# State-space stage: the last doubling of the power tables shared between GpSimd and VectorE, kernel weights written by ScalarE

## The reference, cut to what matters

```
def s4d(x, log_dt, A_re, A_im, C_re, C_im, D_skip):
    Bb, L, D = x.shape
    dt = jnp.exp(log_dt)
    A = A_re + 1j * A_im
    C = C_re + 1j * C_im
    dtA = dt[:, None] * A
    dC = C * (jnp.exp(dtA) - 1.0) / A
    powers = jnp.exp(dtA[:, :, None] * jnp.arange(L))
    K = 2.0 * jnp.einsum('dn,dnl->dl', dC, powers).real
    ...
    y = jnp.fft.irfft(xf * Kf.T[None], n=n, axis=1)[:, :L]
    return y + x * D_skip
```

## Time and profile before

| | us |
|---|---|
| median of 3 runs (3921.81 to 3928.78) | 3927.72 |
| span of the profiled execution | 3923.9 |
| busy in the span: PE, DVE, ACT, POOL | 3188.6, 2978.2, 2267.9, 1587.3 |
| instructions in the span | 54505 |

### The profile page before, as it was taken

The page is one execution under the profiler, slowest core; times in us unless marked ns, Lnnn a source line. Parts: engine busy times, 40 slices in busy tenths (PEclk is TensorE's granted clock), DMA queues, the critical chain, the costliest instruction groups (busy, mean ns, idle before and its releaser), DMA issues. The chain is left out here.

```text
span 3923.9 us, 54505 instructions
## 1 busy us (share of the span) xinstructions
PE 3188.6 (81%) x17202; PEld 2121.8 (54%) x17202; DVE 2978.2 (76%) x7467; ACT 2267.9 (58%) x2921; POOL 1587.3 (40%) x1268
## 2 busy tenths in 40 slices
PE   7638768777887587877987787689999999958999
PEld 3314334444443344445865555477777777746776
DVE  7799999999999999986679998434444334469888
ACT  4579678888987788882133333133323232347876
POOL 0025556555555466555500000113332323217775
PEclk9868878888888788878999999899999999989999
DMA  8710000000000000002223333643444442330212
GB/s 318 260 42 10 10 8 10 10 12 10 10 10 10 8 10 10 12 5 90 93 54 90 83 93 83 188 129 124 129 131 129 129 129 89 113 119 15 62 54 69
DMA packets 262025, 290.53 MB, mean 74 GB/s; under 512 B 53264, under 2 KB 175782, under 8 KB 260588
## 3 DMA queue, kind: packets, MB, share of 16 engines
q1 hardware_dynamic: 243964, 259.49, 21.9%
q10 hardware_dynamic: 14736, 12.89, 1.0%
q0 software_dynamic: 3040, 14.94, 1.0%
HBM read 218.82 MB, written 68.45 MB: 73 GB/s over the span
## 5 line engine op out<-in xcount | busy, mean ns | idle before, releaser
L1119 PE MATMUL up<-ctx,attnT 128*128 128x384 f32 (+1 forms) x1664 | 717.2, 587 | 45.5 <-ACT attnT L989 45.5
L1089 PE MATMUL score<-KT,q 64*128 64x512 f32 (+1 forms) x1792 | 380.2, 518 | 336.9 <-ACT S L949 246.2
L850 DVE MAX8 both_wide<-S 128x8 f32<-128x146 f32 (+1 forms) x2816 | 601.2, 295 | 44.0 <-ACT S L949 24.7
L809 POOL TENSOR_TENSOR S<-S 128x512 f32<-128x512 f32 (+1 forms) x224 | 424.6, 1928 | 355.1 <-DVE S L855 355.1
L1119 PEld LDWEIGHTS up<-ctx,attnT 128*128 128x128 f32 (+1 forms) x1664 | 366.1, 231 | 322.0 <-issue 162.5
L855 DVE SCALAR_TENSOR_TENSOR S<-S,both_wide 128x3202 f32<-128x3202 f32 x128 | 472.8, 3757 | 14.6 <-ACT both_wide L980 14.6
L1089 PEld LDWEIGHTS score<-KT,q 64*128 64x128 f32 x1792 | 172.3, 235 | 535.1 <-ACT S L949 399.9
L949 ACT ACTIVATE S<-score 128x1024 f32<-128x1024 f32 (+1 forms) x448 | 402.7, 931 | 90.3 <-PE score L1089 90.0
L2242 DVE TENSOR_TENSOR ff_gelu<-ff_whole,ff_gelu 128x512 fp32r<-128x512 f32 x128 | 100.5, 785 | 426.6 <-ACT ff_gelu L2436 426.6
L958 ACT ACTIVATE both_wide<-S,below 128x3202 bf16<-128x3202 f32 x128 | 379.7, 2967 | 43.3 <-DVE below L890 22.5
L980 ACT ACTIVATE both_wide<-S,ebias 128x3202 f32<-128x3202 f32 x128 | 376.3, 2964 | 23.9 <-DVE S L855 13.5
(11 more groups left out here) (435 smaller groups left out, 5982.4 us busy)
## 6 DMA issues: line engine op xcount, KB each, us to landing
s_hankel<-scratch_K SPq DMA_DIRECT2D x128, 256.0 KB, 4.4
ff_w_low<-scratch_w1l SPq DMA_DIRECT2D x112, 256.0 KB, 2.6
ff_w_low<-scratch_w2l SPq DMA_DIRECT2D x112, 256.0 KB, 2.7
xt_prep<-in_x SPq DMA_DIRECT2D x8, 1024.0 KB, 8.5
scratch_xt<-xt_prep SPq DMA_DIRECT2D x8, 1024.0 KB, 8.1
both_wide<-in_ffn_w_t POOLq DMA_DIRECT2D x8, 1024.0 KB, 11.0
q<-scratch_qt SPq DMA_DIRECT2D x128, 64.0 KB, 1.9
mod_xt<-in_x_turned SPq DMA_DIRECT2D x32, 256.0 KB, 2.6
```

Of the source, the lines that this page charges most:

```text
L809: nc.gpsimd.tensor_tensor(S[:, b, 0, chunk(j)], S[:, b, 0, chunk(j)], S[:, b, 1, chunk(j)], ALU.add).then_inc(s["summed01"], 1)
L850: nc.vector.max(cand[:, h, 8 * k:8 * k + 8], S[:, b, h, k * SEG:min((k + 1) * SEG, G)])
L1089: last = nc.tensor.matmul(score[bank(p, j)][:, e, 0:w], lhsT=q[at, b, part, h // 2, :], rhs=KT[at, h // 2, chunk(j)], start=(part == 0), s ...
L1119: last = nc.tensor.matmul(up[:, 0:DV], lhsT=attnT[0:w, e, c - 4 * g, :], rhs=ctx[0:w, c, :], start=(c == 0), stop=(c == GC - 1))
```

## The change

It does four things.

1. In the last level of `table(g)`, VectorE forms only the columns 96 to 127 (from 32 to 63). GpSimd forms the columns 64 to 95 (from 0 to 31) in a new function `upper_half(g)`, in four pieces of 8 columns: two multiplications of 128 x 256, a drain, a subtraction and an addition of 128 x 128, a drain. It starts when VectorE has done the level before (`Q_low`) and ends with `Q_upper`, for which `gather(g)` on PE waits beside `Q_ready`.
2. GpSimd's order becomes: weights of part 0, `chunk_turn(0)`, `upper_half(2)`, `upper_half(3)`, then for G = 1 to 6 `upper_half(2G + 2)`, `chunk_turn(G)`, `upper_half(2G + 3)`, and `chunk_turn(7)`.
3. The kernel weights of the parts 1 to 15 are written by ScalarE, four activations after the two `Krow` copies of the part before, and ahead of its last `copy_states`.
4. The bf16 identity is made at the start of `feed_forward` and not at the start of the program (this makes room for the tile `crossed`).

```diff
+    UPPER = 8
...
+        crossed = sb("s4_crossed", [P, 2, GP, UPPER])
...
-                def kernel_weights(g):
+                def first_weights():
 
                     pool.drain()
-                    if g:
-                        pool.wait_ge(s["K_done"], g)
...
+                def upper_half(g):
+
+                    table, at, half = Q[g % RING], pairs(g), P // 2
+                    pool.wait_ge(s["Q_low"], g - 1)
+                    for first in range(0, 2 * PIECE, UPPER):
+                        source, to = table[:, :, :, first:first + UPPER], table[:, :, :, half + first:half + first + UPPER]
+                        for part, into in ((0, to), (1, crossed[:])):
+                            nc.gpsimd.tensor_tensor(into, source, W[:, LEVELS - 1, part, at].unsqueeze(1).unsqueeze(3).broadcast_to([P, 2, GP, UPPER]), ALU.mult)
+                        pool.drain()
+                        nc.gpsimd.tensor_tensor(to[:, 0], to[:, 0], crossed[:, 1], ALU.subtract)
+                        last = nc.gpsimd.tensor_tensor(to[:, 1], to[:, 1], crossed[:, 0], ALU.add)
+                        pool.drain()
+                    last.then_inc(s["Q_upper"], 1)
+
                 pool.drain()
-                kernel_weights(0)
+                first_weights()
                 chunk_turn(0)
-                for g in range(1, PARTS):
-                    kernel_weights(g)
-                    if g % 2 and g > 1:
-                        chunk_turn(g // 2)
+                upper_half(2)
+                upper_half(3)
+                for G in range(1, PARTS // 2 - 1):
+                    upper_half(2 * G + 2)
+                    chunk_turn(G)
+                    upper_half(2 * G + 3)
+                chunk_turn(PARTS // 2 - 1)
...
                         n = 1 << level
-                        for first in range(0, n, 2 * PIECE):
+                        if level == LEVELS - 1:
+                            last.then_inc(s["Q_low"], 1)
+                        for first in range(2 * PIECE if level == LEVELS - 1 else 0, n, 2 * PIECE):
...
+                def kernel_weights(g):
+
+                    for part in range(2):
+                        for e in range(2):
+                            at = slice(NS * e, NS * (e + 1))
+                            last = nc.scalar.activation(Kz[at, part, :, e:e + CHUNKS * (SIDE - 1) + 1:CHUNKS],
+                                                        root[at, part, pairs(g)].rearrange("p (r j) -> p r j", j=SIDE),
+                                                        ACT.Copy, scale=-1.0 if part else 1.0)
+                    last.then_inc(s["Kz_ready"], 1)
...
                     nc.scalar.activation(Krow[:, P - 1:P], ksp[:, 0:1], ACT.Identity, bias=skip[:, g:g + 1]).then_inc(s["K_row"], 1)
+                    if g + 1 < PARTS:
+                        kernel_weights(g + 1)
                     copy_states(g, UG - 1)
...
                     pe.wait_ge(s["Q_ready"], g + 1)
+                    if g >= 2:
+                        pe.wait_ge(s["Q_upper"], g - 1)
...
-                nc.gpsimd.tensor_copy(const["ident_bf"][:], const["ident"][:]).then_inc(ident_made, 1)
-                pool.wait_ge(ident_made, 2)
```

More of the change, by code:

```diff
@@ L1468, in s4d @@
         s = {n: sem("s4_" + n) for n in (
-            "skip_in", "row_set", "Kz_ready", "Q_ready", "turned", "QT_ready", "U_done", "UT_ready", "U_turned", "U_copied", "turn_ready",
+            "skip_in", "row_set", "Kz_ready", "Q_low", "Q_ready", "Q_upper", "turned", "QT_ready", "U_done", "UT_ready", "U_turned", "U_copied", "turn_ready",
             "K_done", "K_row", "K_stored", "h_in0", "h_in1", "h_in2", "h_in3", "h_used", "S_ready", "y_done", "yT_ready", "y_turned",
@@ L1544, in kernel_weights @@
                             last = nc.gpsimd.tensor_scalar(Kz[at, part, :, e:e + CHUNKS * (SIDE - 1) + 1:CHUNKS],
-                                                           root[at, part, pairs(g)].rearrange("p (r j) -> p r j", j=SIDE),
+                                                           root[at, part, pairs(0)].rearrange("p (r j) -> p r j", j=SIDE),
                                                            -1.0 if part else 1.0, None, ALU.mult)
@@ L1923, in feed_forward @@
         zero = sb("ff_zero", [P, DC], BF16)
+        ident_bf = sb("ff_ident_bf", [P, P], BF16)
         edge = sb("ff_edge", [1, 1])
@@ L1938, in feed_forward @@
             "out_wanted", "out_ready", "out_normed", "x_ready", "x_wanted", "x_root", "x_read", "q_ready", "q_turned", "qT_ready",
-            "xt_free", "qT_stored", "rowstep_stored", "x_stored", "x_shifted", "biased", "edges", "rowstep_ready", "rowstep_turned", "rowstep_row", "passed")}
+            "xt_free", "qT_stored", "rowstep_stored", "x_stored", "x_shifted", "ident_bf_made", "biased", "edges", "rowstep_ready", "rowstep_turned", "rowstep_row", "passed")}
         def low_loads(F):
@@ L2064, in _ @@
             def _(pool):
+                nc.gpsimd.tensor_copy(ident_bf[:], const["ident"][:]).then_inc(s["ident_bf_made"], 1)
                 nc.gpsimd.memset(edge[:], 0.0)
@@ L2529, in turn_q @@
                     n = QUAD * g + k
+                    if n == 0:
+                        pe.wait_ge(s["ident_bf_made"], 1)
                     pe.wait_ge(s["q_ready"], n + 1)
@@ L2538, in turn_q @@
                         last = nc.tensor.transpose(fl[k % 2 if g == QUADS - 1 else 1][:].bitcast(BF16)[:, c * P:(c + 1) * P], q[:, k, c * P:(c + 1) * P],
-                                                   const["ident_bf"][:])
+                                                   ident_bf[:])
                     last.then_inc(s["q_turned"], 1)
@@ L3151, in xattn_ffn @@
         const = {"ident": sb("ident", [P, P]), "ones": sb("ones", [P, 1]),
-                 "eps": sb("eps", [P, 1]),
-                 "ident_bf": sb("ident_bf", [P, P], BF16)}
+                 "eps": sb("eps", [P, 1])}
         ident_made = sem("ident_made")
```

## The result

The changed kernel takes 3961.14 us (median of 4 runs, 3957.26 to 3963.57), the kernel before 3925.35 us in the same job (4 runs): a ratio of 1.0091 with a 95% interval of 1.0077 to 1.0106, or **+35.8 us**. The prediction was 3972 us (3945 to 3992), slower with a chance of 0.86. It was right in direction, range and mechanism; the sum of +44.7 was 9 us too large. One of the 16 runs of the kernel before that stand beside the last experiments took 10168.67 us at a granted clock of 0.482, and is left out of their median.

What follows compares the result with a forecast made beforehand. DVE was taken to set the period, with 5 to 7 us a pair before PE. Growth of the tables and pairs, +45.1, less 0.3 to 0.4 at the start, gave +44.7: 3927.7 + 44.7 = 3972 us; range 3945 to 3992.

Steps and rivals of the forecast that it cites:

- T: The begin of a table's last level, where GpSimd may start; the prediction counts its steps in us from there.
- left-overs of the odd table: POOL's nine remaining instructions of an odd table slow the next table's small DVE instructions: +2.6 us.
- Taking turns: DVE and POOL alternate at SBUF reads, one for one; a piece costs DVE 1.41 us; forecast 3954 to 3985, chance 0.72.
- the +5.6 of the even table: Carry after an even table waits for turn factors behind `upper_half`: starts at T + 13.9 instead of T + 8.25.
- without a visible delay of DVE: Claim that POOL's small weights and turn factors, reading 16 to 96 elements, passed beside DVE without visibly slowing it.
- The carry waits for GpSimd: Sign in the profile: DVE gap before each even carry, ended by POOL's `s_turn`, 5 us or so each, seven of them.
- The states as the next wait: At the carry, states come 5.9 us later and DVE's and POOL's path 6.7 us later, so nearly level.
- up to 0.8 us a pair: Cost of the kernel weights on ScalarE, delaying the last `copy_states`, if the turn factors were on time.
- No delay: Rival: POOL's reads do not delay DVE, half tables run at full speed; 3920 us, not slower, chance 0.09.
- Holding for the whole instruction: Rival: the SBUF port is held for the whole instruction, pairs grow by 11.3 us; 4005 us, chance 0.06.
- Only in pauses: Rival: POOL gets in only when DVE pauses, carry at T + 15.7; 3949 us, chance 0.07.
- The best case: Most the edit could give: 4.08 us off all tables until PE is the bound; 3886 us, chance 0.05 with what lies near.

Runs made afterwards that it cites:

- the quarter: Changed kernel with turn factors ahead of the even table's share, GpSimd forming only 16 of the last 64 columns and VectorE 48; 3934.86 us, ratio 1.0020.
- the side work: Changed kernel, but VectorE forms whole tables and GpSimd runs sixteen two-input SBUF instructions a table that nobody waits for; 4010.78 us, ratio 1.0213.
- the memset run: Changed kernel with turn factors first and `upper_half` made one memset that reads nothing; 3883.15 us, ratio 0.9889.

## Why the prediction was right, and 9 us too large

The stage's own growth can be read from the starts of the tables. Within it the profiles give +36.2 us up to `gather(15)`, and the prediction's steps give +45.1. (The stage began 1.8 us earlier and what follows it took 2.8 us less, which is the size of variation between runs and part of the 0.4 us for the identity.)

| step | predicted | measured |
|---|---|---|
| DVE's half ends | T + 6.6 or 6.7 | T + 6.7 (2117.73 to 2124.40) |
| `Q_upper`, even table | T + 12.0 | T + 11.2 |
| `Q_upper`, odd table | T + 13.3 | T + 11.2 |
| T to carry, even table | 13.9, +5.6 | 13.2, +5.0 in five pairs, +4.6 in that of table 6 |
| left-overs of the odd table | +2.6 | +1.7 to +2.6, mostly +2.3 (table 6: start to T 13.26, was 10.96) |
| odd table | -1.5 | -1.3 to -2.1 (table 7: 17.75, was 19.82) |
| pair of table 6 | +6.7 | +5.2 |
| tables 2 and 3, with their left-overs | +2.2 | +1.1 |
| first pair | +4.1 | +2.5 |
| pairs 2 to 5 | +26.8 | +22.5 (5.2, 5.6, 5.7, 6.0) |
| pair 6 to T of table 15 | +8.2 | +7.1 |
| T to `gather(15)` | +3.8 | +3.1 |

- **Taking turns** held, and so did its price, 1.41 us for a piece: 1.45 measured by itself, 1.28 in the quarter. Eight instead of seven of POOL's instructions fitted into DVE's half, one sum more. That makes the rest of the share shorter, and `Q_upper` 0.8 us earlier than predicted.
- **The mis-sized term is the +5.6 of the even table.** It was 0.6 us too large, because `Q_upper` and with it the turn factors came earlier. In the pair of table 6 it was 1.0 too large: I took the carry of before at T + 8.25, which holds for five of the six even tables, but there it waited 0.51 us and began at T + 8.6. A wait that is replaced has to be taken off the price of the one that replaces it. The six even tables are 4.1 of the 9 us (29.5 instead of 33.6), and `gather(15)` is 0.7. The seven left-overs are another 2.5.
- **The rest, about 2 us, is in the odd tables and in table 4.** Up to T these tables had lasted 11.2 to 11.7 us in the kernel before, and lasted 11.0 in the changed one, but for one of 11.4. In table 7 of the kernel before, GpSimd's turn factors ran beside it, and a pair of VectorE's multiplications of 256 elements took 0.94 us there and 0.76 elsewhere. So the prediction's "without a visible delay of DVE", said of the weights and turn factors, was wrong; it bears on no term but this:

```profile
2168.61 0.94 DVE L1581 TENSOR_TENSOR s_M<-s_Q,W 128x256 f32<-128x256 f32 x2
2168.81 0.46 POOL L1557 COPY s_turn<-powers 128x96 f32<-128x96 f32 x1
```

- **The carry waits for GpSimd** was right, in place (L1639), count (seven) and releaser (`s_turn`); it was 6.5 us each, where I had written "5 us or so".
- **The states as the next wait** was right: with the turn factors first six carries wait for ACT. In the changed kernel, the last state copy ends 2.9 us ahead of the carry, so the slack was wider than the tie I described. The prediction let the gather of an odd table start at about T + 13.3, taking GpSimd's last nine instructions as slowed by VectorE; it started at T + 11.3, and the states came 2 us earlier for it. The weights' four activations (0.93 us) hid in that slack. Where the turn factors are on time they cost between 0 and 7 us in all; "up to 0.8 us a pair", 4.8 for six, is inside that.
- **DVE's multiplication** was to grow to some 1.1 us where POOL works; a round of four took 3.93 instead of 2.50 us, so about 1.0 each.
- **The rivals.** No delay (3920) is refuted by 829 ns in place of 687, and by the side work. Holding for the whole instruction (4005) would end DVE's half at T + 8.2; it ended at T + 6.7. Only in pauses (3949) would end it at T + 4.2.
- The best case, 3886, was reached at 3883 by the run whose share reads nothing.

In sum, the 35.8 us are: -42.6 that the shorter level is worth; about +15 for the turn factors behind `upper_half`; and +63 for GpSimd's reads and for its slowness together (3946.5 against 3883.2). (These add up to 35.4; the kernel before was 0.4 us apart in the two jobs.) The +63 was not split further: the same instructions both hold DVE and deliver late.

## What to carry to other kernels

Before work goes from VectorE to GpSimd, price what GpSimd's instruction takes from VectorE, not only how long GpSimd needs. Here a piece of 8 columns took 1.3 to 1.45 us from VectorE, which would have spent 1.05 on it itself, so that a share of the large columns did not pay even where nobody waited for it. What paid (-20 us) was handing over small instructions whose fixed cost is most of their time, at a place where VectorE is at small work too; the size was varied at this place, the place itself was not. And a queue has an order: what others wait for (six small copies) goes ahead of long work that is needed later; that alone was 15 us.

## What the runs showed of the hardware that I had not expected

- A GpSimd instruction with one SBUF input costs VectorE a fifth of one with two (1.2 against 5.8 us a table), although it lasts longer: 847 ns at least for `tensor_scalar` of 256 elements, 0.64 us for `tensor_tensor` alone. Whether it is the input or the kind of instruction is open.
- A GpSimd instruction that only writes costs VectorE nothing: the memset of 1024 elements lasts 0.97 us beside it, and VectorE's products keep 687 ns. Here the run's expectation had it so.
- PE's granted clock moved with its idle time in this stage: 0.90 with 59 us of waiting for tables, 0.94 with 33, 0.97 with 2.3 (the waits in the whole stage). Within the changed kernel, PE's part of a gather that had no wait ahead of it lasted 15.4 us at 1.00, and behind a wait of 8 to 11 us 16.9 to 18.0 us at 0.84 to 0.91. So a gain of VectorE that does away with the wait can bring the states forward by some 2 us more than itself, as in three of six pairs of the memset run.
